# Attention and routing in one kernel: Q's load and the evictions of the last turns first, the probabilities' tile, and the first turn's splits

## What is computed

```python
x = _layernorm(x + _L0_attn_ref(x, ...))  # linear attention over the 256 columns, from Gram products
x = _layernorm(x + _L0_ffn_ref(x, ...))   # softmax gate over 8 experts, gate >= 0.1, sum of x @ expert_w[e]
x = _layernorm(x + _L1_attn_ref(x, ...))  # per row: 16 heads attend to each other
x = _layernorm(x + _L1_ffn_ref(x, ...))   # top 75% of 2048 rows by a score: gelu(x @ w_block)
```

```python
scores = jnp.einsum('bnhd,bngd->bnhg', q, k) / SCALE
attn = jax.nn.softmax(scores, axis=-1)
out = jnp.einsum('bnhg,bngd->bnhd', attn, v)
```

## Time and profile before

| what | us |
|---|---|
| median of 3 runs (lowest to highest) | 1373.98 (1372.45 to 1375.73) |
| the profiled execution's own time | 1370.22 |
| its span, first to last instruction | 1368.3 |
| PE busy, products | 1168.1 (85%) |
| DVE busy | 934.5 (68%) |
| ACT busy | 722.7 (53%) |
| POOL busy | 579.6 (42%) |

### The profile page before, as it was taken

One profiled execution on the slowest core, in us unless ns is written; L12 is line 12 of the kernel. 1 busy time (PEld: TensorE's weight loads), 2 busy tenths in 40 slices (PEclk: granted clock), 3 DMA queues, 4 the chain that ended last, 5 costly groups with the idle time before them and its releaser, 6 DMA issues.

```text
span 1368.3 us, 31179 instructions
## 1 busy us (share of the span) xinstructions
PE 1168.1 (85%) x12264; PEld 749.3 (55%) x12264; DVE 934.5 (68%) x2116; ACT 722.7 (53%) x1146; POOL 579.6 (42%) x886
## 2 busy tenths in 40 slices
PE   6588898998989899998999899998989988995643
PEld 4444456655665556655665546555656544653532
DVE  3544677577866867677866867677766867657845
ACT  3222475347753575447753575537853575545434
POOL 3135335435435446336344356245354345252242
PEclk8799998899979998899979998799978998698556
DMA  5000091205702193203902084202902066108230
GB/s 185 16 2 15 31 158 15 78 9 114 111 9 71 32 172 31 79 8 99 126 2 78 17 175 43 79 9 82 143 2 63 1 154 63 38 26 151 37 93 31
DMA packets 93145, 90.64 MB, mean 66 GB/s; under 512 B 7110, under 2 KB 81864, under 8 KB 92744
## 3 DMA queue, kind: packets, MB, share of 16 engines
q1 hardware_dynamic: 80648, 75.54, 29.7%
q0 software_dynamic: 2560, 8.39, 1.8%
q10 hardware_dynamic: 9792, 4.72, 1.5%
HBM read 46.68 MB, written 41.94 MB: 65 GB/s over the span
## 4 chain that ended last, share of the span: by engine, by line
PE 38%; DVE 20%; POOL 11%; ACT 10%; DMA 9%; issue 8%; SPq 3%; ACTq 1%; POOLq 0%; DVEq 0%
PE bank L1848 36%; DMA ct<-scratch_qkv 4%; POOL stage L647 4%; SPq L520 3%; DVE keys L1546 2%; DMA bt<-scratch_o 2%; ACT shared L796 2%; DMA scratch_o<-stage 2%; DVE x L1435 2%; DVE stats L1294 2%; POOL rs L597 2%; DVE gelu L1548 2%; DVE ct L1264 1%; ACT x L920 1%; PE bank L1858 1%
## 5 line engine op out<-in xcount | busy, mean ns | idle before, releaser
L1848 PE MATMUL bank<-we,at 128*128 128x512 f16 x1536 | 372.2, 401 | 1.9 <-DVE x L1435 1.9
L1848 PEld LDWEIGHTS bank<-we,at 128*128 128x128 f16 x1536 | 154.0, 102 | 193.5 <-issue 40.0
L612 POOL TENSOR_TENSOR part<-part 128x512 f32<-128x512 f32 x64 | 83.7, 1308 | 273.3 <-ACTq L946 273.3
L796 ACT ACTIVATE part<-bank,wexp 128x256 f32<-128x256 f32 x256 | 104.6, 472 | 162.7 <-PE bank L1848 108.6
L1435 DVE SCALAR_TENSOR_TENSOR x<-bank,wexp,x 128x256 f32<-128x256 f32 x256 | 122.7, 479 | 53.5 <-PE bank L1848 47.0
L1848 PE MATMUL bank<-bt,wqkv 128*128 128x512 f16 x576 | 138.8, 383 | 21.3 <-DVE stage L1264 15.6
L920 ACT ACTIVATE x<-x,nm,rs 128x256 f32<-128x256 f32 x192 | 104.6, 593 | 90.8 <-POOL nm L600 89.6
L1264 DVE TENSOR_TENSOR stage<-bank,stage 128x512 f16<-128x512 f32 x112 | 75.6, 686 | 83.8 <-ACT stage L796 83.6
L593 POOL TENSOR_SCALAR nm<-mv 128x2 f32<-128x2 f32 x128 | 35.3, 276 | 226.6 <-DVE mv L1299 220.9
L1848 PE MATMUL bank<-keys,blockdiag 128*128 128x16 f16 x3072 | 97.1, 193 | 19.7 <-issue 15.6
L1848 PEld LDWEIGHTS bank<-keys,blockdiag 128*128 128x128 f16 x3072 | 95.7, 104 | 24.4 <-issue 22.8
(11 more groups left out here) (189 smaller groups left out, 2247.9 us busy)
## 6 DMA issues: line engine op xcount, KB each, us to landing
scratch_qkv<-stage SPq DMA_DIRECT2D x40, 512.0 KB, 3.3
ct<-scratch_qkv SPq DMA_DIRECT2D x112, 128.0 KB, 7.1
x_in<-in_x_dram SPq DMA_DIRECT2D x32, 256.0 KB, 2.8
keys<-scratch_qkv SPq DMA_DIRECT2D x64, 128.0 KB, 6.1
bt<-scratch_o SPq DMA_DIRECT2D x16, 512.0 KB, 3.7
out_dram<-x POOLq DMA_DIRECT2D x32, 256.0 KB, 2.7
scratch_qkv<-part SPq DMA_DIRECT2D x8, 512.0 KB, 8.3
scratch_o<-stage SPq DMA_DIRECT2D x32, 128.0 KB, 3.6
```

The costliest lines, as they stand in the source:

```text
L612: pool.tensor_tensor(part[:, 0:2, :], part[:, 0:2, :], part[:, 2:4, :], ALU.add)\
L796: return act.activation(dst, src, ACT.Copy, scale=scale)
L1848: ins = pe.matmul(dst, lhs, rhs, start=(n == 0), stop=(n == len(terms) - 1))
```

## The change

1. `probs_t` becomes a function of the batch: a view of `xs` for batches 0 to 6, of `ct` for batch 7. The wait for `v_turned` in ACT's `b_pt` goes.
2. In `closing`, DVE evicts F0 to F7 before anything of batch 6's ranks, and only comparisons 0 and 1 stay there, between F8 and F11. Comparisons 2 and 3 move to `ending` behind the second `b_ssum`, 4 to 7 with bound and selection behind the last eviction of O. The scores of batch 6 move to a part of `we` (`scores_of`). PE's sums for the ranks follow, behind O3. POOL's `b_res` goes; ACT does it in `ending`, and batch 6's Gelus move there too.
3. SP issues its four loads of batch 7's Q ahead of the store of F4 and F5.
4. Batch 6's stores on POOL and two of ACT's last normalisings of it move behind steps of batch 7.
5. First turn: DVE takes two of POOL's four splits of x, the weights' splits 1 to 3 move behind `a_ap(a, 1)` and 4 to 6 behind `a_ap(a, 2)`, and PE waits for them just ahead of the gate. The two bias rows are split where the last group was.

The core of the diff:

```diff
-        probs_t = ct[:, :, :, :].rearrange("p k l n -> p (k l n)").rearrange("p (l c m) -> p l c m", l=2, c=16)
+        def probs_t(b):
+            home = flat_ct if b == NB - 1 else flat_xs
+            return home.rearrange("p (l c m) -> p l c m", l=2, c=16)
...
+        def scores_of(b):
+            return flat_we[:, 2 * C + 28 * P:4 * C + 28 * P].bitcast(fp32) if b == NB - 2 else scores
...
             def load_x(a, p):
-                    sp.wait_ge(xs_lo, 4 * (a - 1) + p + 1)
+                    sp.wait_ge(xs_lo, 4 if a == 1 else 4 * (a - 1) + p + 1)
...
             def b_loads(b):
                 b_f(b, 1)
                 b_f(b, 3)
+                b_loadq(b)
                 b_f(b, 5)
-                b_loadq(b)
                 b_f(b, 7)
...
-            def b_res(b, p):
-                pool.wait_ge(ranked, b + 1)
...
             def b_pt(b, q):
                 act.wait_ge(b_full, b_filled(b, f"PT{q}"))
-                if b < NB - 1:
-                    for hf in range(2):
-                        act.wait_ge(v_turned[hf], b + 1)
-                copy(pt_part(q, HI), b_ps(f"PT{q}")).then_inc(pt_hi, 1)
+                copy(pt_part(b, q, HI), b_ps(f"PT{q}")).then_inc(pt_hi, 1)
...
# ACT, ending
                 for p in range(TP):
-                    b_ffn(c, p)
+                    b_gelu(c, p)
+                for p in range(TP):
+                    b_res(c, p)
+                b_ffn(c, 0)
+                b_ffn(c, 1)
                 for p in range(TP):
                     b_prn(b, p)
                 for p in range(TP):
                     b_tz(b, p)
+                b_ffn(c, 2)
+                b_ffn(c, 3)
...
# DVE, start
+            for p in (1, 3):
+                pair = slice(2 * p, 2 * p + 2)
+                dve.wait_ge(xs_hi, p + 1)
+                split_lo(xs[:, pair, LO, :], x_in[:, pair, :], xs[:, pair, HI, :]).then_inc(xs_lo, 1)
```

More of the change, by code:

```diff
@@ L773, in ending @@
                 for p in range(TP):
+                    ln(b, p, 1)
+                for p in range(TP):
                     b_store(c, p)
-                for p in range(TP):
-                    ln(b, p, 1)
                 for p in range(TP):
@@ L781, in ending @@
                 b_store(b, TP - 1)
-            for p in range(TP):
+            for p in (0, 2):
                 a_xs(0, p)
@@ L907, in b_rout @@
                 act.wait_ge(late_full(b, f"ROUT{h}"), late_filled(b, f"ROUT{h}"))
-                copy(scores[:, 512 * h:512 * (h + 1)], late_ps(b, f"ROUT{h}")).then_inc(late_free(b, f"ROUT{h}"), 1)
+                copy(scores_of(b)[:, 512 * h:512 * (h + 1)], late_ps(b, f"ROUT{h}")).then_inc(late_free(b, f"ROUT{h}"), 1)
             def b_ff(b, p):
@@ L1553, in b_bound @@
                 dve.wait_ge(compared, T * (b + 1))
[L1554 to L1557 removed]
+                dve.tensor_reduce(rank[:, :], rowsum[:, :, :], X, ALU.add).then_inc(bounded, 1)
+                dve.wait_ge(bounded, 2 * b + 1)
+                dve.tensor_tensor(rank[:, :], rank[:, :], keep_less_after, ALU.add).then_inc(bounded, 1)
+                dve.wait_ge(bounded, 2 * b + 2)
             def b_select(b):
@@ L1641, in turn @@
                     a_norm(a)
-                if b is None and c is None:
-                    split_weights(range(1, 4))
                 if b is not None:
@@ L1658, in turn @@
                 if b is None and c is None:
-                    split_weights(range(4, N_SPLITS))
+                    split_rows()
                 if c is not None:
@@ L1702, in turn @@
                     a_ap(a, 1)
+                if b is None and c is None:
+                    split_weights(range(1, 4))
                 if b is not None:
@@ L1722, in turn @@
                     a_ap(a, 2)
+                if b is None and c is None:
+                    split_weights(range(4, N_SPLITS))
                 if b is not None:
@@ L1817, in ending @@
                     b_o(b, q)
+                for t in range(4, T):
+                    b_rank(c, t)
+                b_bound(c)
+                b_select(c)
                 for p in range(TP):
@@ L2210, in turn @@
                     b_f(b, 10)
+                if b is None and c is None:
+                    pe.wait_ge(w_hi, N_SPLITS + 1)
+                    pe.wait_ge(w_lo, N_SPLITS + 1)
                 if a is not None:
@@ L2256, in closing @@
                 b_tx(b, 3)
-                b_f(b, 0)
-                b_f(b, 1)
                 b_tz(c, 3)
-                b_f(b, 2)
-                b_f(b, 3)
+                for k in range(4):
+                    b_f(b, k)
                 b_rout(c, 1)
@@ L2268, in closing @@
                 b_f(b, 7)
-                b_f(b, 8)
-                b_f(b, 9)
+                for k in range(8, 12):
+                    b_f(b, k)
                 b_ff(c, 2)
                 b_ff(c, 3)
-                b_f(b, 10)
-                b_f(b, 11)
-                b_rank(c, 0)
-                b_rank(c, 1)
             def ending(b, c):
```

73 lines of the change are left out of this document (28 added, 45 removed).

## The result

| | before | after |
|---|---|---|
| median, us (lowest to highest, runs) | 1372.45 (1366.59 to 1375.73, 9) | 1358.97 (1354.74 to 1362.97, 9) |
| ratio, 95% interval | | 0.9902, 0.9883 to 0.9921 |
| the profiled execution's time, span | 1370.22, 1368.3 | 1357.91, 1356.1 |
| PE busy | 1168.1 | 1167.6 |

The change is faster by 1.0%. The forecast of 1363.6 was 4.6 us too high, inside its range. PE's products take as long as before, so what went is idle time of PE: 12.2 us of the span, 10.4 by the sum.

A forecast was written before the change was run, and what follows sets the result against it. PE was taken as the spine, with 38% of the chain that ended last. Gains of 7.3 + 2.6 + 0.5 = 10.4 us off 1370.22 gave 1359.8, plus 3.8 for the median 1363.6; range 1357 to 1369.5.

The forecast's parts named there:

- the sum: Whole kernel: gains of middles, last turns and first turn added up, 10.4 us less.
- The middles: Middle of seven turns: without ACT's wait for V's turning, S3 starts earlier, 7.3 us gained together.
- The last turns: End of the kernel: V 0.5 us later, DVE turning V first worth 3.1, together 2.6 us gained.
- V half a microsecond later: Last turns: K's load and so V's arrival come 0.5 us later, V at 1279.3.
- at that rate it takes 10 us: Last turns: Q's 1 MB loads at one queue's 105 GB/s, from about 1240.3, ahead of two stores and K.
- two queues double Q: Rival, last turns: two queues load Q in 5 us, K and V come 4 us earlier, 1359.6 us; chance 0.28.
- The full DMA share: Last turns: a share of 1.26 at 105 GB/s was taken to show the DMA engines full, favouring one rate.
- DVE first is worth 3.1: Last turns: DVE copies its half of V ahead of POOL, ending at V + 2.5 instead of V + 5.9.
- the scalings on ACT cost and bring nothing: Last turns: ACT does Gelus and eight scalings, some 6 us, in POOL's place; cost 0 to 0.6, taken as 0.
- The first turn: First turn: moved splits gain 4.2 us up to line 1357, most is given back behind it; net 0.5 gained.
- The losses that the sum named: First turn: splits beside POOL's normalising steps cost 1.5 us, `gw`, `wrt`, `ebd` ahead of the statistics 2.2.
- The 3.8 us that were added for the median: Total: the runs' median of 1373.98 stood 3.8 above the profiled execution, so this was added to 1359.8.

The follow-up runs named there:

- first_only: The kernel before with only the change's first turn (x split on two engines, weights' splits moved): 1371.23 us, ratio 0.9984.
- mid_only: The kernel before with only the probabilities of all batches but the last put into `xs`, without ACT's wait: 1366.17 against 1373.78 us, ratio 0.9952.
- change_again: The changed kernel run once more without any edit, beside later kernels: 1355.18 us, ratio 0.989 to the kernel before.
- pool_first: The changed kernel with one added wait, so DVE copies its half of the last V only after POOL's half: 1357.6 us, 0.9881 to the kernel before.
- q_order: The kernel before with one line moved, SP issuing its half of Q's load ahead of the third store: 1371.59 against 1370.18 us, ratio 1.0011.
- last_only: The kernel before with only the change's last turns (Q's load earlier, comparisons behind the evictions, scalings on ACT): 1370.15 us, ratio 0.9983.
- first_holes: The changed kernel with the first turn's weight splits placed where DVE and POOL both wait: 1355.61 us, 0.9898 to the kernel before.
- v_act: The changed kernel with ACT instead of POOL turning the second half of the last batch's V: 1355.73 against 1370.18 us, 0.989 to the kernel before.

## Why the prediction was right, and where not

**The middles: right, in the mechanism and the size.** 7.3 us were forecast, 39.64 - 32.38 = 7.26 went. S3 starts 1.56 us behind the maxima (1.55 forecast), these 0.04 us behind S2's end, in each of the seven turns. In the last it is 2.08 us less and in the first 1.72 (2.1 and 1.7 forecast), in the second nothing. What made it exact is that the new bound was built from rows of steps that the change doesn't touch, not from the wait that it removes: the 15.9 us of ACT's waits would have promised twice as much.

**The last turns: the sum about right, two terms wrong in opposite directions.** 2.6 us forecast, 2.3 measured alone. *V half a microsecond later* was wrong: in eight executions with this part V's load is issued 23.20 to 26.31 us behind ACT's half of Q, against 28.25 (27.99 and 28.99 in `first_only` and `mid_only`), so 1.9 to 5.1 us earlier. The step that failed is "at that rate it takes 10 us": with the start that is 11.7 us from ACT's first issue to Q's last landing, and it took 10.2 in the profile of the change and 8.0 in `change_again`. K's load followed 9.96 to 12.84 us behind ACT's half, where the sum has 14.8 and its rival 10.7. (Both have a slip: their own terms end at 1252.9 and 1247.9, not at 1253.4 and 1249.3.) In the profile of the change the two halves of Q move at 114, then 150 GB/s (stretches: length, busy time of PE, PEld, DVE, ACT, POOL, then granted clock, DMA share, GB/s), and the two stores, beside Q's last piece, at 328; then K's load:

```profile
1229.00:1233.00 4.00, 3.67 (x18) 1.48 (x16) 1.71 (x5) 1.79 (x3) 0.00 (x0) 1.00 1.24 114
1233.00:1236.00 3.00, 2.40 (x11) 0.77 (x10) 3.00 (x8) 0.60 (x1) 0.00 (x0) 1.00 1.34 150
1236.00:1239.00 3.00, 3.00 (x26) 2.31 (x25) 0.65 (x4) 0.58 (x2) 0.00 (x0) 1.00 0.87 328
1242.00:1249.00 7.00, 0.00 (x0) 0.00 (x0) 6.96 (x11) 6.86 (x4) 0.00 (x0) 0.50 1.25 108
```

and in `change_again`, the same kernel, at 200 with K's load behind at 117:

```profile
1229.00:1233.00 4.00, 3.33 (x16) 1.26 (x14) 1.93 (x5) 1.79 (x3) 0.00 (x0) 1.00 1.20 200
1238.00:1245.00 7.00, 1.38 (x13) 0.98 (x11) 6.96 (x9) 6.97 (x4) 0.00 (x0) 0.98 1.22 117
```

So neither one rate nor twice the rate: the rival "two queues double Q" was half right, differently in each execution. The full DMA share, on which I had leaned, is 1.25 at 108 GB/s and 1.20 at 200 and says nothing on the rate. *DVE first is worth 3.1* was wrong as well: `pool_first` and `change_again` give it 0.5 and 0.1. The step that failed looked at DVE's copy alone and not at its next instruction, the spread, which POOL's copy then holds up (4.12 us instead of 0.75). And *the scalings on ACT cost and bring nothing* missed that POOL's silence gives the spreads of Q 3.0 us back; without that, and without batch 6's steps out of the way, V's earlier load is worth nothing (`q_order`). From ACT's half of Q to the heads' outputs it is 55.47 to 56.83 us in the three executions without this part and in `q_order`, and 51.66 to 53.73 in the five that have it and leave V's second half to POOL, 3.6 less in the mean. That the sum's 2.6 came out near this is luck: one term was too small and one too large.

**The first turn: the sum stands, within a noise larger than itself.** Forecast 4.2 gained up to line 1357 and 3.7 given back behind it. The one pair of profiles above says 5.8 and 6.8, but it is not typical. Four executions have the old first turn (`before`, `mid_only`, `last_only`, `q_order`) and six the change's:

| us, mean (lowest to highest) | old first turn, 4 | the change's, 6 |
|---|---|---|
| start of PE | 9.49 (9.43 to 9.64) | 8.88 (8.20 to 9.58) |
| start of line 1357 | 48.52 (48.09 to 48.96) | 43.91 (42.81 to 44.62) |
| start of the experts' products | 76.09 (74.52 to 78.49) | 75.65 (74.90 to 76.81) |

So 4.6 us are gained up to line 1357, 0.6 of them at the start of PE (0.7 forecast), and 4.2 given back; the 0.4 that stay, 0.5 by the sum, can't be told from nothing where single executions differ by up to 4 us. The losses that the sum named, POOL beside the splits and `ebd` ahead of the statistics, are worth some 3 by `first_holes` (3.7 forecast). Much of the difference between executions goes with the granted clock. From line 1357 to the experts' products the old first turn takes 26.1 us in the two executions where the clock was 0.84 in 43 to 58 us, and 28.6 and 29.5 in the two where it was 0.64 and 0.61, with no edit in that turn. The kernel before, then `last_only`:

```profile
43.00:58.00 15.00, 9.08 (x48) 6.67 (x46) 11.35 (x24) 4.36 (x11) 1.60 (x5) 0.84 0.12 35
43.00:58.00 15.00, 10.85 (x41) 7.93 (x42) 10.71 (x21) 4.39 (x10) 0.00 (x0) 0.61 0.12 35
```

At 0.84 four executions of the change's first turn take 31.2 to 31.4 us there, 5.2 more than the old one, so at that clock it gives back more than the sum had. That the clock itself costs these microseconds is read from such pairs; no run sets it apart.

**The clock in the ending** took 1.5 us in this pair: the router's 12 products last 4.84 us in the change, 3.37 before. It changes with the execution, as 3.31 in `first_holes` and 4.38 in `first_only`, which doesn't touch the last turns, show. But it may lean with the change too: the four executions with the old ending have 3.26 to 3.37 and once 4.38, the eight with the new one 4.24 to 4.84 and once 3.31. That is not enough to show it, and the sum had no term for it. The products in the profile of the change:

```profile
1323.12 4.84 PE L1852 MATMUL bank<-ct,wrt 128*128 128x512 f16 x12 [0.56 <-DVE ct L1263]
```

**The total.** 12.3 us between the two profiled executions, 10.4 by the sum. The places above give 7.3 (middles), 3.0 (from the end of `closing` to the heads' outputs of the last batch), -1.0 (first turn) and -1.5 (router): 7.8. The other 4.4 us lie in stretches ahead of the last turns in which nothing of the change stands. The same 24 products of the experts behind S1 took 6.31 to 7.97 us in the kernel before and 6.35 to 7.92 in the change, 50.1 and 48.2 us for the seven; and the two profiled executions of the change differ by 3.7 us in span. I read this as the difference of two executions. The twelve executions bear it out: from the first S of batch 0 to that of batch 6 it is 934.6 to 938.7 us in the four with the old middles and 925.4 to 932.0 in the eight with the new ones. The means differ by 6.5 us and the six middles in between by 5.5, so what the middles save arrives, and the rest is within what executions differ by. The 3.8 us that were added for the median rested on three runs; with nine it is 2.2. That is 1.5 of the 4.6 us by which the forecast was too high; the other 3.1 are the gain, 13.5 against 10.4. The chance of 0.90 for faster rested on the middles, the one term that the runs show in mechanism and size.

## What to carry to other kernels

Cost a removed wait by the next bound at its place, built from steps that the change leaves alone, and check it in every repetition: here seven times 4.62 us came out of two rows. When DVE and POOL work on the same memory, look at the pair of instructions on both sides of the overlap: who wins the copy loses the next step, and the remedy is to give the work to ACT or to a place where one of the two waits. Gains of 3 us at one place of a kernel whose executions differ by 9 can be proved at the place, by distances between two events of one timeline, and hardly in the total. Even there one pair of profiles can mislead: for the first turn it said 1.0 us lost, and all that were profiled say 0.4 gained, within their noise.

## What the runs showed of the hardware

- DVE's float16 copies and spreads and POOL's copies of 128x2048 exclude each other whole: 2.48 and 5.93 us or 5.91 and 3.83 for the same pair, and 16.0 to 16.1 us up to the heads' outputs either way. DVE's splits (two operands from memory) hold up POOL's small steps too: 1.70 instead of 0.20 us, 2.61 instead of 0.71. ACT's copy of the same tile beside DVE's is no such case: 3.84 and 2.49 us in `v_act`, where DVE's alone took 2.43 (`pool_first`).
- Two queues that load 16 partitions at a time each moved 114 to 200 GB/s over four microseconds in nine executions, one queue in K's load behind them 102 to 131. The Trainium skill, "SBUF — State Buffer", section "Can I just issue two DMAs to hit both halves?", saw hardly more from two transfers than from one; the three executions at 114 and 115 agree, the one at 200 doesn't. What decides it was not found. It goes along with the issues: where they lay 0.3 us apart it was 114 to 138 (four executions), where they coincided 128 to 200 (five).
- The granted clock of the same products at the same place of the program differs from one execution to the next (3.26 to 4.84 us for twelve of the router), so a difference of one such piece between two profiles need not be an effect of an edit.
